# Third stage of a four-layer graph network: feed-forward and head scores in fp32r passes over parts, residual by transposes, end of the layer norm on VectorE, last attention first in the step

## The chip, the cores and the metric

One core of one Trainium2 chip. The metric is the time of one execution in device microseconds; the median of three runs is given beside the lowest and the highest. TensorE multiplies, VectorE, ScalarE and GpSimd work on SBUF (the first two on PSUM as well), SyncE issues the transfers.

## The reference

`x` is 64 graphs of 128 nodes with 256 features, `adj` one 128 x 128 matrix. Four residual blocks run one after the other, each on `h = relu(layernorm(x))`: an attention with 8 heads, a linear mixing with degrees, a graph attention with 4 heads and feed-forward (the third stage, which the change touches), and a graph attention with one head.

```python
def heads(x, adj, W, a):                       # W: [H, F, O], a: [H, 2O]
    Wh = einsum('bnf,hfo->bhno', x, W)
    f1 = einsum('bhno,ho->bhn', Wh, a[:, :O])
    f2 = einsum('bhno,ho->bhn', Wh, a[:, O:])
    e = f1[:, :, :, None] + f2[:, :, None, :]
    e = where(e > 0, e, 0.01 * e)
    e = where(adj > 0, e, -1e9)
    return einsum('bhnm,bhmo->bhno', softmax(e), Wh)

h = elu(heads(h, adj, W_heads, a_heads))       # 4 heads of 256
out = elu(heads(h.reshape(B, N, 1024), adj, W_out, a_out))
y = relu(out @ w1 + b1) @ w2 + b2 + out
x = x + layernorm(y) * ln_gamma + ln_beta
```

## The kernel before

All of `x` lies in SBUF (`x_all`). Every stage works through 32 groups of two graphs (G = 2) in a software pipeline: `run_steps` calls the stage's step function for t = -2 up to 35, and within a step each engine has a fixed, hand-written order of pieces that belong to different groups. In the third stage (`step2` of each engine) the pieces have a lag: `f` (group t) transposes h, forms the head features and scores of the four heads; `m` (group t-1) is the softmax's transposes and the four heads' attention; `o2` (t-2) is the product with W_out; `l` (t-3) is the last attention and the first feed-forward product; `e` (t-4) is the second feed-forward product, the residual and the layer norm. Only steps 4 to 31 hold all five. Engines meet by semaphores alone; there is no planner.

Large products run in fp32r over parts: an operand w is split into `w_hi` (a copy rounded to fp32r) and `w_lo` (the rest), and hi*hi + lo*hi + hi*lo are summed in PSUM, three passes in the place of one fp32 product (L1324 projections, L1350 W_out, L1311 features). In the trace an fp32 product shows as two matmul records. The feed-forward products (L1433, L1372) and the head scores (L1393) are plain fp32.

TensorE's order in a step before: transposes of h (L1141), transposes of probs (L1366), second feed-forward product with uT as the stationary operand (L1372) and the residual, outT times the identity (L1374), features, head(0) and head(1) (L1337), head scores with the mask (L1390, L1393), last scores (L1147, L1401), out_product(0) and (1) (L1350), project(0) (L1324), head(2), transposes of the last probabilities (L1412), out_product(2), head(3), last attention (L1422), project(1), out_product(3), first feed-forward product (L1433). PSUM bank 7 is used by the last scores, the last attention, both feed-forward products and y in turn, so each piece waits until the one before it was read.

VectorE's pieces: `hT2_lo` (L721), low_head (L697), y from bank 7 plus b2 (L729), `left`, `right_rows`, `right` for the head scores (L735, L736, L739), elu_head (L690, L692), bn_stats and bn_aggr (L746, L756; L248, L263 for the next h), soft (L702, L704), the last softmax (L760, L762, L769, L772), normalise (L708, L710), the ELU of the last attention `em3` and `outT` (L793, L797), the scaling of y (L784), `wh2` (L717). ScalarE's: `hT2_hi` (L997), probsT (L993), high_head (L973), exp_head (L966), scores_out (L979), exp_scores (L985), project_out (L960), h (L291), the last attention's copies and exponentials (L1017, L1026, L1042, L1058), uT (L1073). GpSimd does the square roots (L277, L489), adds beta to x (L304), multiplies y by gamma (L494) and adds it to x (L497).

Of the kernel before, what the change touches and what calls it, by code (L numbers as in the profile page):

```python
# [13 lines left out]
FP32 = mybir.dt.float32  # L14
# [55 lines left out]
def build_program(nc, x, adj, L0_gnn_Wq, L0_gnn_bq, L0_gnn_Wk, L0_gnn_bk, L0_gnn_Wv, L0_gnn_bv, L0_gnn_Wo,  # L70
# [10 lines left out]
    with ctx:  # L81
# [10 lines left out]
        ffn2 = sb("ffn2", [N, KC, D])  # L92
        w3 = sb("w3", [N, KC, F3 + 2])
        consts = sb("consts", [N, N + 4 + H2 * N])
# [3 lines left out]
        head_rows = consts[:, N + 4:].rearrange("p (h n) -> p h n", h=H2)  # L98
# [16 lines left out]
        bv_wide = sb("bv_wide", [N, KC, N])  # L115
# [17 lines left out]
        hT = sb("hT", [N, KC, G, N])  # L133
# [7 lines left out]
        rwide0 = sb("rwide0", [N, 4, 4 * DH])  # L141

        left = sb("left", [64, N])
        right_rows = sb("right_rows", [64, N])
        right = sb("right", [64, H2, N])
# [10 lines left out]
        em3 = sb("em3", [N, KC, G, N])  # L156
        outT = sb("outT", [N, KC, G, N])
        uT = sb("uT", [N, KC, G, N])
        y = sb("y", [N, G, D])
# [4 lines left out]
        h3 = sb("h3", [N, 4, G, F3 + 2])  # L164
# [6 lines left out]
        with ExitStack() as early:  # L171
# [6 lines left out]
            with ExitStack() as layer0:  # L178
# [10 lines left out]
                att0T = sb_0("att0T", [N, KC, G, N])  # L189
            with ExitStack() as layer1:  # L190
# [14 lines left out]
        wf_hi = sb("wf_hi", [N, KC, 3 * DH], F32R)  # L205
        wf_lo = sb("wf_lo", [N, KC, 3 * DH], F32R)
# [8 lines left out]
        a3_rows = h3[:, 0, :, 0:F3]  # L215
# [156 lines left out]
        u_full = sem("u_full")  # L372
        u_ready = sem("u_ready")
        y_full = sem("y_full")
# [3 lines left out]
        yg_ready = sem("yg_ready")  # L378
# [53 lines left out]
        LATE_DONE = 4 + 4 * H2 + 8 + 4  # L432
# [21 lines left out]
        def _(pool):  # L454
# [25 lines left out]
            if PHASES > 2:  # L480
                pool.wait_ge(pre[1].x, NG)

                def step2(at):
# [23 lines left out]
        def _(dve):  # L507
# [45 lines left out]
            def late_part(i):  # L553
# [8 lines left out]
                if i in (1, 2):  # L562
                    s = i - 1
                    for hh in range(H2):
                        late(nc.vector.tensor_tensor(prod4, wh[:, :, hh, :], av[:, hh, s:s + 1, :].broadcast_to([N, KC, D]), ALU.mult))
                        late(nc.vector.reduce_sum(wh_f[:, :, s * H2 + hh], prod4, AX.X))
                if i in (0, 3):
# [113 lines left out]
            def step2(at):  # L681
# [41 lines left out]
                if o2:  # L723
                    low_head(3, go)
                if e:
                    dve.wait_ge(y_full, ge + 1)
                    if positive(ge):
                        dve.wait_ge(pre[2].x, ge)
                    nc.vector.tensor_tensor(y[:, :], bank[7][:, :].rearrange("p (c d) -> p c d", c=G),  # L729
                                            b2_row[:, :, :].broadcast_to([N, G, D]), ALU.add).then_inc(y_step, 1)  # L730
                if f:
# [6 lines left out]
                    dve.wait_ge(lr_step, g * 2 + 1)  # L738
                    nc.vector.tensor_tensor(right[:, :, :], right_rows[:, :].unsqueeze(1).broadcast_to([64, H2, N]),  # L739
                                            head_rows[0:64], ALU.mult).then_inc(lr_step, 1)  # L740
                if m:
                    elu_head(0)
                if e:
# [3 lines left out]
                    last.then_inc(y_step, 1)  # L747
                if m:
# [9 lines left out]
                if l:  # L758
                    dve.wait_ge(scores3, gl + 1)
                    nc.vector.scalar_tensor_tensor(t3[:, 0], t3[:, 0], LEAK2, t3[:, 0], ALU.mult, ALU.max).then_inc(top3, 1)  # L760
                    dve.wait_ge(top3, gl * 2 + 1)
                    nc.vector.tensor_reduce(negtop[:, :], t3[:, 0], AX.X, ALU.max, negate=True).then_inc(top3, 1)  # L762
# [4 lines left out]
                if l:  # L767
                    dve.wait_ge(exp3, gl + 1)
                    nc.vector.reciprocal(rsum3[:, :], sum3[:, 0, :]).then_inc(rsum3_ready, 1)  # L769
                    dve.wait_ge(rsum3_ready, gl + 1)  # L770
                    for c in range(G):
                        last = nc.vector.tensor_scalar(t3[:, 0, c, :], t3[:, 0, c, :], rsum3[:, c:c + 1], None, ALU.mult)  # L772
                    last.then_inc(p3_ready, 1)
                if f:
                    normalise(0)
                moments_dve(2, at)
                if m:
                    low_head(0, gm)
                    low_head(1, gm)
                    elu_head(2)  # L780
                if e:
                    dve.wait_ge(y_norm, ge * 2 + 2)
                    for c in range(G):
# [3 lines left out]
                if f:  # L787
                    normalise(1)
                if m:
                    elu_head(3)  # L790
# [728 lines left out]
```

## Time and profile before

| | us |
|---|---|
| median of 3 runs | 1637.37 (1637.23 to 1638.43) |
| the profiled execution | 1637.47 |
| its span | 1635.7 |
| TensorE busy | 1449.0 (89%) |
| VectorE busy | 1202.6 (74%) |
| ScalarE busy | 1024.2 (63%) |
| GpSimd busy | 454.5 (28%) |

Busy time is the union of an engine's instructions, as a share of the span. Durations of matmuls are pipelined: two that follow one another overlap, so the time that one occupies is read from start to start. A row of a timeline merges a few like instructions (x8) and gives in brackets the idle time before it and what ended it.

### The profile page before, as it was taken

Reading aid. Unit: us, or ns where it says so; the run is one execution under the profiler, and the core shown is the slowest. Engines: PE = TensorE matmul, PEld = TensorE weight load, DVE = VectorE, ACT = ScalarE, POOL = GpSimd, SP = SyncE. Lnnn points to the kernel's source line nnn. Section 1 sums busy time; section 2 is a strip of 40 time slices with the busy share of each in tenths; the row PEclk is TensorE's granted clock in tenths of the full one; section 3 lists DMA queues with packets and bytes.
Section 4 is the critical chain, followed back from the end, with each engine's and each line's share of the span. In section 5 each row is a group of like instructions: output and inputs, shape, how many; then the busy total and the mean of one; then the engine's idle time right before and its main releaser. Section 6 shows DMA issues by size and latency. Waiting matters only on the chain.

```text
span 1635.7 us, 36230 instructions
## 1 busy us (share of the span) xinstructions
PE 1449.0 (89%) x11581; PEld 1276.4 (78%) x11645; DVE 1202.6 (74%) x2747; ACT 1024.2 (63%) x3241; POOL 454.5 (28%) x747
## 2 busy tenths in 40 slices
PE   5689999999879987999999999999999999965776
PEld 4578888888769985888888888888888888854554
DVE  4877777767657766777878787787878778743887
ACT  3568878878735546666656566665656666522776
POOL 1122222222036652122223132222313222122332
PEclk9889999999969997999999999999999999996999
DMA  7400000000000000000000000000000000000112
GB/s 238 136 2 0 0 0 0 0 0 0 1 1 0 0 0 1 1 1 1 1 0 0 0 0 0 0 0 0 0 0 0 0 0 1 1 1 7 65 64 71
DMA packets 23873, 24.23 MB, mean 15 GB/s; under 512 B 1936, under 2 KB 23184, under 8 KB 23696
## 3 DMA queue, kind: packets, MB, share of 16 engines
q1 hardware_dynamic: 23824, 23.60, 4.6%
q8 instruction: 27, 0.44, 0.1%
q14 instruction: 22, 0.18, 0.0%
HBM read 15.21 MB, written 8.39 MB: 14 GB/s over the span
## 4 chain that ended last, share of the span: by engine, by line
PE 43%; DVE 26%; ACT 17%; issue 12%; DVEq 1%; POOL 1%; DMA 0%; ACTq 0%; SPq 0%; POOLq 0%
ACT probs L877 9%; PE bank L1433 4%; DVE em L690 4%; PE bank L1337 4%; PE bank L1372 4%; PE bank L1141 3%; DVE probs L702 2%; PE bank L1234 2%; PE bank L1225 2%; DVE st L248 2%; PE bank L1393 2%; PE bank L1266 2%; PE bank L1279 2%; PE bank L1278 2%; PE bank L1280 2%
## 5 line engine op out<-in xcount | busy, mean ns | idle before, releaser
L877 ACT ACTIVATE probs<-bank,negtop 128x128 f32<-128x128 f32 x512 | 185.8, 415 | 48.0 <-DVE negtop L630 48.0
L275 POOL TENSOR_TENSOR var_eps<-mv,eps_tile 128x2 f32<-128x2 f32 x128 | 48.5, 379 | 590.7 <-DVE mv L263 590.7
L291 ACT ACTIVATE h<-x_all,shift,rstd 128x256 f32 (+1 forms) x256 | 140.0, 597 | 33.1 <-POOL shift L281 33.1
L1350 PE MATMUL bank<-wout_hi,headsT_hi 128*128 128x258 f32 x512 | 150.5, 294 | 0.0
L1350 PE MATMUL bank<-wout_lo,headsT_hi 128*128 128x258 f32 x512 | 144.4, 282 | 0.0
L1350 PE MATMUL bank<-wout_hi,headsT_lo 128*128 128x258 f32 x512 | 144.2, 282 | 0.0
L966 ACT ACTIVATE em<-bank 128x512 f32<-128x512 f32 x128 | 75.7, 591 | 98.9 <-PE bank L1337 98.5
L487 POOL TENSOR_TENSOR var_y<-mv_y,eps_tile 128x2 f32<-128x2 f32 x32 | 8.8, 276 | 463.1 <-DVE mv_y L756 463.1
L1337 PE MATMUL bank<-probsT,whs 128*128 128x128 f32 x1024 | 132.8, 278 | 0.0
L877 ACT ACTIVATION_READ_ACCUMULATOR probs<-bank,negtop 128x1 f32 x512 | 130.0, 254 | 0.0
L1337 PEld LDWEIGHTS bank<-probsT,whs 128*128 128x128 f32 x1024 | 125.9, 194 | 2.7
L985 ACT ACTIVATE probs<-probs,negtop 128x128 f32<-128x128 f32 x256 | 99.9, 394 | 27.8 <-DVE negtop L704 27.8
L690 DVE TENSOR_SCALAR em<-em 128x512 f32<-128x512 f32 x128 | 85.2, 666 | 33.4 <-ACT em L966 29.9
L277 POOL TENSOR_TENSOR rstd<-var_eps,pow_half 128x2 f32<-128x2 f32 x128 | 104.6, 818 | 10.0
L1324 PE MATMUL bank<-wh_hi,hT_hi 128*128 128x512 f32 x256 | 104.7, 409 | 1.4 <-ACT probs L979 1.4
L1183 PE MATMUL bank<-consts,probs 128*128 128x128 f32 x512 | 75.3, 280 | 31.6 <-DVE probsT L586 17.1
L1324 PE MATMUL bank<-wh_hi,hT_lo 128*128 128x512 f32 x256 | 101.8, 398 | 0.0
L1433 PE MATMUL bank<-outT,ffn 128*128 128x256 f32 x256 | 65.5, 400 | 40.8 <-DVE outT L797 40.8
L1324 PE MATMUL bank<-wh_lo,hT_hi 128*128 128x512 f32 x256 | 101.6, 397 | 0.0
L1350 PEld LDWEIGHTS bank<-wout_hi,headsT_hi 128*128 128x128 f32 x512 | 96.8, 189 | 2.4 <-issue 0.8
L1350 PEld LDWEIGHTS bank<-wout_lo,headsT_hi 128*128 128x128 f32 x512 | 97.2, 190 | 1.2
L627 DVE TENSOR_REDUCE negtop<-bank 128x4 f32<-128x512 f32 x128 | 88.4, 690 | 12.1 <-PE bank L1234 12.1
(215 smaller groups left out, 4638.3 us busy)
## 6 DMA issues: line engine op xcount, KB each, us to landing
x_all<-in_x SPq DMA_DIRECT2D x32, 256.0 KB, 2.8
out_x<-x_all SPq DMA_DIRECT2D x32, 256.0 KB, 2.1
wh<-in_L_gnn_W_heads SPq DMA_DIRECT2D x2, 512.0 KB, 7.9
a_heads<-in_L_gnn_a_heads SPq DMA_DIRECT2D x1, 1024.0 KB, 11.1
wout<-in_L_gnn_W_out SPq DMA_DIRECT2D x1, 1024.0 KB, 10.8
raw<-in_L_gnn_W SPq DMA_DIRECT2D x1, 512.0 KB, 5.3
ffn<-in_L_gnn_w SPq DMA_DIRECT2D x2, 256.0 KB, 7.2
consts<-in_shape_consts SPq DMA_DIRECT2D x1, 322.0 KB, 2.8
```

What stands on the lines that cost most here:

```text
L277: nc.gpsimd.tensor_tensor(rstd[:, p, :], var_eps[:, p, :], pow_half[:, :], ALU.pow).then_inc(s.norm, 1)
L291: last = nc.scalar.activation(h[:, p, c, :], x_all[:, bass.ds(g * G + c, 1), :].rearrange("p a d -> p (a d)"), ACT.Relu, bias=shift[:, p, ...
L627: nc.vector.tensor_reduce(negtop0[:, r, :], bank[4 + r][:, :].rearrange("p (k n) -> p k n", k=4), AX.X, ALU.max, negate=True).then_inc(top ...
L690: nc.vector.tensor_scalar(em[:, i % 2], em[:, i % 2], 1.0, -1.0, ALU.min, ALU.add).then_inc(hd2_elu, 1)
L877: last = nc.scalar.activation(probs[:, r, i, :], bank[4 + r][:, i * N:(i + 1) * N], ACT.Exp, bias=negtop0[:, r, i:i + 1], scale=float(DH) ...
L966: nc.scalar.activation(em[:, i % 2], bank[3 + i % 2][:, :].rearrange("p (k n) -> p k n", k=KC), ACT.Exp).then_inc(hd2_exp, 1)
L985: last = nc.scalar.activation(probs[:, c, hh, :], probs[:, c, hh, :], ACT.Exp, bias=negtop2[:, c, hh:hh + 1], accum_out=sum2[:, c, hh:hh + 1])
L1183: last = nc.tensor.transpose(bank[2 + r % 2][:, k * N:(k + 1) * N], probs[:, r, k, :], ident)
L1324: last = nc.tensor.matmul(bank[1 + half][:, :], src[:, k, c, :], w[:, k, 2 * half:2 * half + 2, :].rearrange("p h o -> p (h o)"), start=(k ...
L1337: last = nc.tensor.matmul(bank[3 + i % 2][:, (o * G + c) * N:(o * G + c + 1) * N], whs[:, pm, c, i * D + o * N:i * D + (o + 1) * N], probs ...
L1350: last = nc.tensor.matmul(bank[5 + c][:, 0:D + 2], src[:, i, o, c, :], w[:, k, :], start=(k == 0 and src is headsT_hi and w is wout_hi), s ...
L1433: last = nc.tensor.matmul(bank[7][:, o * G * N:(o + 1) * G * N], ffn1[:, k, o * N:(o + 1) * N], outT[:, k].rearrange("p c n -> p (c n)"), ...
```

## The change

Five things are done to the third stage.

1. ffn1 and ffn2 are split once into hi and lo (in steps 0 and 1, ScalarE the copy, VectorE the rest). `outT` and `uT` are split in every step by VectorE. Both feed-forward products become three fp32r passes each.
2. The residual is four fp32 transposes of outT into bank 7 ahead of the second product, which adds to it; it waits for `uT` alone, the product for its parts.
3. Head scores: the features' weight columns stand twice, so that the 16 rows hold f and f again; VectorE takes `f_high` (rounded), forms `f_part` (f_high in the first rows, f - f_high in the others), and from that `left`, `right_rows` and `right` in fp32r. The product with them is one fp32r pass per graph.
4. The end of the layer norm goes to VectorE: (y - mean) * gamma, then times rstd plus x, each a scalar_tensor_tensor per graph. GpSimd keeps the square roots and the beta add.
5. Order. TensorE: last scores between head(0) and head(1), last probabilities' transposes after out_product(1), last attention after project(0), first feed-forward product ahead of out_product(3). VectorE and ScalarE follow with the pieces of `l` earlier, and exp_scores(0) behind both high_heads, project_out(0) and (1) behind exp_scores(1). The loop's buffers `em3`, `uT`, `outT`, `y` now lie in unused quarters of probs and probsT, `h3` and `hT` in whs.

```diff
 # gpsimd, step2
-                    if there:
-                        pool.wait_ge(yn_ready, g + 1)
-                        nc.gpsimd.tensor_tensor(y[:, :], y[:, :], gamma_row[:, :, :].broadcast_to([N, G, D]),
-                                                ALU.mult).then_inc(yg_ready, 1)
-                        pool.wait_ge(yg_ready, g + 1)
-                        nc.gpsimd.tensor_tensor(x_group(g), x_group(g), y[:, :], ALU.add).then_inc(pre[2].x, 1)
 # vector, step2
-                    nc.vector.tensor_scalar(left[:, :], bank[0][0:64, 0:N], left_mul[0:64], left_add[0:64], ALU.mult, ALU.add)
-                    nc.vector.tensor_scalar(right_rows[:, :], bank[0][0:64, 0:N], right_mul[0:64], right_add[0:64],
+                    nc.vector.tensor_copy(f_high[:, :], bank[0][0:64, 0:N]).then_inc(lr_step, 1)
+                    dve.wait_ge(lr_step, g * 4 + 1)
+                    nc.vector.scalar_tensor_tensor(f_part[:, :], f_high[:, :].bitcast(FP32), low_rows[0:64], bank[0][0:64, 0:N],
+                                                   ALU.mult, ALU.add).then_inc(lr_step, 1)
+                    dve.wait_ge(lr_step, g * 4 + 2)
+                    nc.vector.tensor_scalar(left[:, :], f_part[:, :], left_mul[0:64], left_add[0:64], ALU.mult, ALU.add)
+                    nc.vector.tensor_scalar(right_rows[:, :], f_part[:, :], right_mul[0:64], right_add[0:64],
                                             ALU.mult, ALU.add).then_inc(lr_step, 1)
...
-                if e:
-                    dve.wait_ge(y_norm, ge * 2 + 2)
-                    for c in range(G):
-                        last = nc.vector.tensor_scalar(y[:, c, :], y[:, c, :], mv_y[:, c, 0:1], rstd_y[:, c:c + 1],
-                                                       ALU.subtract, ALU.mult)
-                    last.then_inc(yn_ready, 1)
...
+                    dve.wait_ge(at3_elu, gl * 2 + 2)
+                    nc.vector.tensor_copy(outT_hi[:, :, :, :], outT[:, :, :, :]).then_inc(outT_ready, 1)
+                    dve.wait_ge(outT_ready, gl * 2 + 1)
+                    nc.vector.tensor_tensor(outT_lo[:, :, :, :], outT[:, :, :, :], outT_hi[:, :, :, :].bitcast(FP32),
+                                            ALU.subtract).then_inc(outT_ready, 1)
+                if f:
+                    normalise(0)
+                if m:
+                    elu_head(2)
+                if f:
+                    normalise(1)
+                if m:
+                    elu_head(3)
                     low_head(2, gm)
+                if l:
+                    dve.wait_ge(u_relu, gl + 1)
+                    nc.vector.tensor_copy(uT_hi[:, :, :, :], uT[:, :, :, :]).then_inc(u_ready, 1)
+                    dve.wait_ge(u_ready, gl * 2 + 1)
+                    nc.vector.tensor_tensor(uT_lo[:, :, :, :], uT[:, :, :, :], uT_hi[:, :, :, :].bitcast(FP32),
+                                            ALU.subtract).then_inc(u_ready, 1)
+                if e:
+                    dve.wait_ge(y_step, ge * 3 + 3)
+                    for c in range(G):
+                        last = nc.vector.scalar_tensor_tensor(y[:, c, :], y[:, c, :], mv_y[:, c, 0:1], gamma_row[:, 0, :],
+                                                              ALU.subtract, ALU.mult)
+                    last.then_inc(yn_ready, 1)
+                    dve.wait_ge(yn_ready, ge + 1)
+                    dve.wait_ge(y_norm, ge * 2 + 2)
+                    dve.wait_ge(pre[2].bias, ge + 1)
+                    for c in range(G):
+                        xs = x_all[:, bass.ds(ge * G + c, 1), :].rearrange("p a d -> p (a d)")
+                        last = nc.vector.scalar_tensor_tensor(xs, y[:, c, :], rstd_y[:, c:c + 1], xs, ALU.mult, ALU.add)
+                    last.then_inc(pre[2].x, 1)
 # tensor, step2
+                def residual():
+                    pe.wait_ge(u_relu, ge + 1)
+                    for c in range(G):
+                        for k in range(KC):
+                            nc.tensor.matmul(bank[7][:, c * D + k * N:c * D + (k + 1) * N], outT[:, k, c, :], ident, is_transpose=True,
+                                             start=(c == 0 and k == 0), stop=False)
+
+                def second_ffn():
+                    pe.wait_ge(u_ready, ge * 2 + 2)
+                    for c in range(G):
+                        for k in range(KC):
+                            for src, w in ((uT_hi, ffn2_hi), (uT_hi, ffn2_lo), (uT_lo, ffn2_hi)):
+                                last = nc.tensor.matmul(bank[7][:, c * D:(c + 1) * D], src[:, k, c, :], w[:, k, :], start=False,
+                                                        stop=(c == G - 1 and k == KC - 1 and src is uT_lo))
+                    last.then_inc(y_full, 1)
...
+                def first_ffn():
+                    if not positive(gl):
+                        pe.wait_ge(w_lo, 5)
+                    pe.wait_ge(outT_ready, gl * 2 + 2)
+                    for o in range(KC):
+                        for k in range(KC):
+                            for w, src in ((ffn1_hi, outT_hi), (ffn1_lo, outT_hi), (ffn1_hi, outT_lo)):
...
```

## Rows read from the trace of the kernel before

**Rows 1.** Busy time by engine in one stretch of the third stage:
```profile
core 0: us, PE busy (x) PEld busy (x) DVE busy (x) ACT busy (x) POOL busy (x), PEclk, DMA share, GB/s
700.00:1300.00 600.00, 567.62 (x3928) 501.66 (x3950) 481.73 (x993) 376.93 (x1059) 167.13 (x207) 1.00 0.00 0
```

**Rows 2.** Timeline of GpSimd over one step, start us and length us first:
```profile
1000.66 1.29 POOL L494 TENSOR_TENSOR y<-y,gamma_row 128x512 f32<-128x512 f32 x1 [1.40 <-DVE y L784]
1002.14 1.50 POOL L497 TENSOR_TENSOR x_all<-x_all,y 128x512 f32 x1 [0.19 <-POOL y L494]
...
1019.55 1.42 POOL L304 TENSOR_TENSOR x_all<-x_all,beta_row 128x512 f32 x1
...
1026.68 1.29 POOL L494 TENSOR_TENSOR y<-y,gamma_row 128x512 f32<-128x512 f32 x1 [1.40 <-DVE y L784]
```

**Rows 3.** Two lines of the third stage: count, ns min/median/max, first and last start:
```profile
L721 DVE TENSOR_TENSOR hT_lo<-bank,hT_hi x32: 682/692/692, 617.5 to 1399.4; 128x512 fp32r<-128x512 f32 x32
...
L729 DVE TENSOR_TENSOR y<-bank,b_row x32: 690/692/693, 699.6 to 1481.7; 128x512 f32<-128x512 f32 x32
```

**Rows 4.** Waits between 700 and 1300 us: total, times, longest:
```profile
ACT uT L1073 <- PE bank L1433: 67.5, 23, 3.0
DVE hT_lo L721 <- ACT hT_hi L997: 57.5, 23, 2.5
...
PE bank L1433 <- DVE outT L797: 30.3, 23, 1.3
```

**Rows 5.** Timeline of TensorE over one step:
```profile
1005.77 1.99 PE L1433 MATMUL bank<-outT,ffn 128*128 128x256 f32 x8 [1.33 <-DVE outT L797]
1007.60 0.60 PE L1141 MATMUL bank<-consts,h 128*128 128x128 f32 x4
...
1008.91 1.03 PE L1372 MATMUL bank<-ffn,uT 128*128 128x256 f32 x4
...
1011.45 0.30 PE L1311 MATMUL bank<-hT_hi,wf_hi 128*64 128x128 f32 x1
...
1014.65 1.13 PE L1393 MATMUL bank<-right,left 32*128 32x512 f32 x4
1015.71 0.43 PE L1147 MATMUL bank<-consts,wh 128*128 128x128 f32 x2
...
1016.01 0.36 PE L1350 MATMUL bank<-wout_hi,headsT_hi 128*128 128x258 f32 x1
...
1018.96 0.39 PE L1324 MATMUL bank<-wh_hi,hT_hi 128*128 128x512 f32 x1
```

**Rows 6.** Timeline of VectorE over one step:
```profile
999.86 0.73 DVE L784 TENSOR_SCALAR y<-y,mv_y,rstd_y 128x256 f32<-128x256 f32 x2
...
1000.71 1.79 DVE L710 TENSOR_TENSOR probs<-probs,rsum 128x512 f32<-128x512 f32 x1
1002.42 1.51 DVE L690 TENSOR_SCALAR em<-em 128x512 f32<-128x512 f32 x1
...
1004.57 0.42 DVE L793 TENSOR_SCALAR em<-em 128x512 f32<-128x512 f32 x1
...
1012.55 0.40 DVE L735 TENSOR_SCALAR left<-bank,consts 64x128 f32<-64x128 f32 x1
...
1018.36 0.40 DVE L760 SCALAR_TENSOR_TENSOR t<-t 128x256 f32<-128x256 f32 x1
...
1021.42 0.48 DVE L772 TENSOR_SCALAR t<-t,rsum 128x128 f32<-128x128 f32 x2
...
1022.02 0.69 DVE L710 TENSOR_TENSOR probs<-probs,rsum 128x512 f32<-128x512 f32 x1
```

**Rows 7.** Group of a line in the set-up: count, busy us, mean ns, idle before:
```profile
L531 DVE CAST wkT_hi<-bank 128x512 fp32r<-128x512 f32 x1 | 0.7, 692 | 0.0
```

**Rows 8.** Chain that ended last, in the drain of the third stage:
```profile
1477.07 2.08 PE bank L1372 x4
...
1481.72 0.70 DVE y L729
...
1485.38 1.27 POOL y L494
```

More of the change, by code:

```diff
@@ L140, in build_program @@
         rsum0 = sb("rsum0", [N, 4, 4])
-        rwide0 = sb("rwide0", [N, 4, 4 * DH])
-        left = sb("left", [64, N])
+        left = sb("left", [64, N], F32R)
+        f_high = sb("f_high", [64, N], F32R)
+        f_part = sb("f_part", [64, N])
         right_rows = sb("right_rows", [64, N])
-        right = sb("right", [64, H2, N])
+        right = sb("right", [64, H2, N], F32R)
         negtop2 = sb("negtop2", [N, G, H2])
@@ L155, in build_program @@
         p3T = sb("p3T", [N, G, N])
[L156 to L159, printed above, removed]
+        outT_hi, outT_lo, uT_hi, uT_lo = [sb(name, [N, KC, G, N], F32R) for name in ("outT_hi", "outT_lo", "uT_hi", "uT_lo")]
         st_y = sb("st_y", [N, G, 6])
@@ L730, in step2 @@
                                             b2_row[:, :, :].broadcast_to([N, G, D]), ALU.add).then_inc(y_step, 1)
+                if o2:
+                    low_head(3, go)
                 if f:
@@ L810, in step2 @@
                     nc.vector.tensor_tensor(flat(wout_lo), flat(wout), flat(wout_hi).bitcast(FP32), ALU.subtract).then_inc(w_lo, 1)
+                if isinstance(at.t, int) and at.t == 1:
+                    for i, (w, hi, lo) in enumerate(((ffn1, ffn1_hi, ffn1_lo), (ffn2, ffn2_hi, ffn2_lo))):
+                        dve.wait_ge(w_hi, 4 + i)
+                        nc.vector.tensor_tensor(flat(lo), flat(w), flat(hi).bitcast(FP32), ALU.subtract).then_inc(w_lo, 1)
             if PHASES > 2:
@@ L1050, in step2 @@
                         nc.scalar.copy(hi, w).then_inc(w_hi, 1)
+                if n and isinstance(gn, int) and gn == 1:
+                    for hi, w in ((ffn1_hi, ffn1), (ffn2_hi, ffn2)):
+                        nc.scalar.copy(flat(hi), flat(w)).then_inc(w_hi, 1)
                 if m:
@@ new lines, in scores @@
+                def scores():
+                    pe.wait_ge(lr_step, g * 4 + 4)
+                    if positive(g):
+                        pe.wait_ge(whs_ready, g * 4)
+                    for c in range(G):
+                        nc.tensor.matmul(bank[1 + c][:, :], ident_bf[:, :], hide2[:, :, :], start=True, stop=False)
+                    for c in range(G):
+                        rows = slice(c * 32, (c + 1) * 32)
+                        nc.tensor.matmul(bank[1 + c][:, :], left[rows, :], right[rows].rearrange("p h n -> p (h n)"),
+                                         start=False, stop=True).then_inc(s2_full, 1)
@@ new lines, in scores_last, with probs_last @@
+                def scores_last():
+                    pe.wait_ge(wh2_act, gl + 1)
+                    pe.wait_ge(wh2_dve, gl + 1)
+                    if positive(gl):
+                        pe.wait_ge(y_step, gl * 3 - 2)
+                    neighbours(bank[7], wh2[:, pl, :, D + 1:D + 2], stop=False)
+                    nc.tensor.matmul(bank[7][:, 0:G * N], ident_bf[:, :], hide2[:, 0:G, :], start=False, stop=True).then_inc(s3_full, 1)
+                def probs_last():
+                    pe.wait_ge(p3_ready, gl + 1)
+                    for c in range(G):
+                        last = nc.tensor.transpose(bank[7][:, c * N:(c + 1) * N], t3[:, 0, c, :], ident)
+                    last.then_inc(pT3_full, 1)
@@ new lines, in attend_last @@
+                def attend_last():
+                    pe.wait_ge(pT3_ready, gl + 1)
+                    for o in range(KC):
+                        for c in range(G):
+                            last = nc.tensor.matmul(bank[7][:, (o * G + c) * N:(o * G + c + 1) * N], wh2[:, pl, c, o * N:(o + 1) * N],
+                                                    p3T[:, c, :], start=True, stop=True)
+                    last.then_inc(at3_full, 1)
+                def first_ffn():
+                    if not positive(gl):
+                        pe.wait_ge(w_lo, 5)
+                    pe.wait_ge(outT_ready, gl * 2 + 2)
+                    for o in range(KC):
+                        for k in range(KC):
+                            for w, src in ((ffn1_hi, outT_hi), (ffn1_lo, outT_hi), (ffn1_hi, outT_lo)):
+                                last = nc.tensor.matmul(bank[7][:, o * G * N:(o + 1) * G * N], w[:, k, o * N:(o + 1) * N],
+                                                        src[:, k].rearrange("p c n -> p (c n)"),
+                                                        start=(k == 0 and w is ffn1_hi and src is outT_hi), stop=(k == KC - 1 and src is outT_lo))
+                    last.then_inc(u_full, 1)
@@ L1368, in step2 @@
                 if e:
-                    pe.wait_ge(u_ready, ge + 1)
-                    for c in range(G):
-                        for k in range(KC):
-                            nc.tensor.matmul(bank[7][:, c * D:(c + 1) * D], uT[:, k, c, :], ffn2[:, k, :], start=(k == 0), stop=False)
-                        for k in range(KC):
-                            last = nc.tensor.matmul(bank[7][:, c * D + k * N:c * D + (k + 1) * N], outT[:, k, c, :], ident,
-                                                    start=False, stop=(k == KC - 1))
-                    last.then_inc(y_full, 1)
+                    residual()
+                    second_ffn()
                 if f:
```

182 lines of the change are left out of this document (82 added, 100 removed).

## The prediction

> **What bounds the kernel now.** I read the windows by stage first. The third stage runs from about 617 to 1488 us, and in its settled middle (700 to 1300 us) TensorE is busy 567.62 of 600 us, VectorE 481.73 and ScalarE 376.93 [rows 1]. Next the timeline of GpSimd, which gives the beat: the gamma product starts at 1000.66 and again at 1026.68 [rows 2], so a step takes 26.02 us, and the 600 us hold 23.06 steps. Per step that is TensorE 24.6 us, VectorE 20.9, ScalarE 16.3. The steps that do everything are steps 4 to 31, 28 of them: the last split of hT starts at 1399.4, in step 31, and 27 beats before it lie at 696.9, just ahead of the first y add at 699.6 [rows 3]. Next the waits [rows 4]: TensorE's one regular wait is for outT ahead of the first feed-forward product, 30.3 us in 23 steps, 1.3 us each. VectorE waits 2.5 us a step for ScalarE's hT_hi, which itself is queued behind uT, for which ScalarE waits 2.9 us on that same product. So the bound is TensorE's queue plus one hole per step, which the chain attention 3 -> outT -> first product -> uT makes at the end of the step. Last the timeline of TensorE, for what each piece occupies [rows 5], and that of VectorE [rows 6]. There two instructions stand out: the normalising product takes 1.79 us at 1000.71 but 0.69 at 1022.02, and the em clamp takes 1.51 at 1002.42 while the like clamp of em3 takes 0.42 at 1004.57 [rows 6]. Each long one ends 0.3 to 0.55 us after a GpSimd product of 512 columns that runs over it (ends at 1001.95 and 1003.64) [rows 2, 6]. VectorE thus loses 1.10 + 1.09 = 2.2 us a step to GpSimd.
>
> **The change part by part: TensorE.** I count from start to start, since the pipelined durations overlap. 24 passes in fp32r of 258 columns take 18.96 - 16.01 = 2.95 us, 0.123 each [rows 5].
> - First product: 7.60 - 5.77 = 1.83 us now; 12 passes of 256 columns give 1.47. Minus 0.36.
> - Second product with residual: 11.45 - 8.91 = 2.54 now. After: 12 passes, 1.47, and 4 transposes; the step's four transposes of h and eight of probs lie between 1007.60 and 1008.91, 0.11 each, so 0.44. Minus 0.63.
> - Head scores: 15.71 - 14.65 = 1.06 now. Two fp32r products of 512 columns on 32 rows aren't in the trace. From below: the two, which stand on different partitions, run wholly beside one another, 0.25; from above: no gain, 1.06. I take two passes behind one another at twice the price of a 256-column one, 0.49. Minus 0.57 (0 to 0.8).
> - The hole of 1.33: the last attention is now begun before the head sums, so outT has more than a step's half to be formed and split. It goes, if VectorE keeps up (below).
> TensorE's step: 26.02 - 1.33 - 0.36 - 0.63 - 0.57 = 23.1 us (22.9 to 23.7).
>
> **VectorE**, from 20.9:
> - Scores by parts: f_high and f_part read PSUM like `left` now (0.40) and each is waited for by the next, so 0.43 each; left and right_rows then read SBUF, where a 128-column scaling costs about 0.28 (the pair at 1021.42 takes 0.48) instead of 0.40 [rows 6]. Plus 0.6 (0.4 to 0.9).
> - Splitting outT and uT: per tile a cast of 512 columns from SBUF to fp32r and a subtraction. The subtraction is like the two-tensor product at 1022.02, 0.69. The cast isn't in the trace. From below: the clamp of 512 columns, SBUF to SBUF, 0.42; from above: a cast from PSUM to fp32r, 0.69 [rows 7]. I take 0.43, since it is the same movement as the clamp, SBUF to SBUF with one tensor read. Plus 1.1 for each tile (to 1.4), 2.2 together.
> - Layer norm end: two scalings go (0.73 the pair, 0.65 by starts); four scalar_tensor_tensor of 256 columns come, the nearest 0.40 for 256, 0.35 by starts. Plus 0.75 (0.6 to 1.1).
> - GpSimd's product with gamma and its add to x go: minus 2.2 of VectorE's stalls. The add of beta stays, 1.42 us. Now it runs over a reduction and bn_stats, which it doesn't stretch. After the change the batch statistics of y end later, and the add falls on low_head(0), a two-tensor subtraction in SBUF, which by my walk is reached 0.65 us before the add ends: plus 0.65 (0 to 1.1).
> Sum: 20.9 + 0.6 + 2.2 + 0.75 - 2.2 + 0.65 = 22.9 us (21.9 to 24.6).
> The Trainium skill (SBUF — State Buffer, on the shared port pair) calls this pair an exclusive lock: the second of a two-input or fast-mode VectorE instruction and a GpSimd one blocks until the first is done. The trace agrees, with 1.79 against 0.69 us, and the rule gives both the stalls that go and the one that comes; if the length had another cause that stays, the sum would be 24.4. The Trainium skill (VectorE: DVE Perf Modes, the perf-mode tier table) gives an fp32 copy in SBUF the double rate but names no fp32r output; by it the casts would be nearer 0.43.
>
> **ScalarE** keeps its instructions, 16.3 us: it is only reordered. GpSimd loses two of its longest.
>
> **The walk of one step.** I laid the new order out by hand with these prices, each engine in its own order, each instruction after what it waits for, from TensorE's transposes of h at 0. For TensorE and the chain: splits of hT done 3.0 (VectorE still ends the previous layer norm until 2.4), second product 1.75 to 3.2, y read 4.1, features to 3.9, last scores at 4.9, `right` done 6.7, just when head(1) ends (6.45: 0.25 us of waiting), p3 ready 9.8 for transposes at 10.3, attention 13.3 to 14.2, em3 at 14.9, outT split by 18 or 18.6 for a product that TensorE reaches at 20.2; uT 22.6, its split until 23.8, which is 0.7 into the next step for a product at 1.75. VectorE's ends, without the stall by the beta add: y 4.1, low_head(3) 4.7, `right` 6.7, maximum of the last scores 7.5, elu_head(0) 8.5, bn_stats of y 9.1, p3 9.8, elu_head(1) 10.9, soft(0) and soft(1) 13.7, bn_stats of x 14.3, low_head(0) and (1) 15.7, outT and its parts 18.0, normalise(0) 18.8, elu_head(2) 19.9, normalise(1) 20.7, elu_head(3) 21.8, low_head(2) 22.3, parts of uT 23.8, end of the layer norm 25.1, wh2 25.4, the last three in the next step's time. Nothing of the moved chain is late, but VectorE runs with no more than 0.4 us of rest. What is late next is therefore VectorE and TensorE in turn: `hT2_lo` ahead of the features, `right` ahead of the scores. 23.1 and 22.9 with 0.3 of such mutual waiting: **a step of 23.4 us**. Queued behind `right` are the hide matmuls, both out products and project(0), so each delay there goes into the beat.
>
> **Fill and drain.** The fill gains 0.6 us a step on the scores and pays 0.8 for the parts in steps 0 and 1, where they are on the path, and a little for splitting ffn1 and ffn2 once; its products and holes gain as above where they have begun: minus 2 in all, an estimate. In the drain I follow the chain [rows 8]. The last step: second product with residual from 1477.07 to 1481.72 at the lower of the two clocks (four products in 2.08 us against 1.03 at 1008.91), 4.65; after it 12 passes at twice the pitch, 2.9, behind a split of 1.1, with the residual beside it: minus 0.6. Behind the square root on GpSimd the scalings (0.8), the gamma product (1.3) and the add (1.3) become one pair of 0.8: minus 2.7. The steps 33 and 34: splits 1.1 each, the second product 0.3 less with its split counted, the first product 0.4 to 1 less, and in 33 the attention no longer behind an out product (1.47 less 0.4 for the copy of p3T it hid): minus 1 for both. Step 32 loses its hole and a stretched clamp: minus 1.5. Together minus 6.
>
> **Sum.** 28 x (26.02 - 23.4) = 73, fill 2, drain 6: minus 81. The profiled execution took 1637.47 us (span 1635.7, so 1.8 outside), the median of the runs is 1637.37; the two are the same to 0.1 us. 1637.5 - 81 = **1556 us**.
>
> **The rivals.**
> 1. VectorE becomes the bound alone: casts at 0.69, scaling with two pointers at 0.40, the full stall by the beta add; the sum 24.6, or about 24.5. For it: 20.9 is already high and this engine gets 10 instructions and loses 2; against: the 2.2 us of stalls are measured. Time: 1637.5 - 28 x 1.5 - 8 = 1587.
> 2. VectorE has room, the scores overlap: TensorE's 22.9 alone. 1637.5 - 28 x 3.1 - 9 = 1542. Against: it wants all of VectorE's prices at their lower end.
> 3. Slower. Bank 7 is one buffer for the whole chain scores 3, attention 3, first product, second product, y; it is passed once a step, and the splits put 2.3 us and four instructions of a full VectorE queue into it. uT's split is behind low_head(2), the second product in front of the features. If it comes late, TensorE stands and everything behind it. The point where it decides: 0.7 into the step by my walk, harmless to 1.75, no gain left if it ends 2.9 us later than that, at 4.6. At 5.6 the beat is 27.0 and the time 1637.5 + 28 x 1.0 - 8 = 1657. Against: in the walk the chain's links are met by their engines with 1 to 2.2 us to spare.
> 4. The parts don't pay: fp32r on 32 rows is no faster than fp32. TensorE 23.7, a step of 23.9: 1570, inside the forecast's range.
>
> **How the numbers follow.** Forecast with rival 4 (a step of 23.1 to 24.0): 0.61. Rival 1: 0.24. Rival 2: 0.08. Rival 3: 0.04. Between 25.5 and 26.1 us a step, no measurable change: 0.03. Range 1538 to 1592: the bounds 22.9 and 24.6 of the two sums, with 2 us beyond; it leaves out rival 3, the no-change case and the tails. About 0.2%, 3 us, is what a measurement can tell from no change. Faster 0.93, same 0.03, slower 0.04.
>
> **What would show it.** The beat of the y add near 23.4. TensorE without a wait at the first product, with short ones at features or scores. VectorE above 95% busy. The normalising product and the clamps at 0.69 and 0.42 without long ones, and low_head(0) stretched under the beta add. The casts at 0.43. A cast at 0.69 or a wait of TensorE for the split of uT would make the prediction wrong.

## The result and the profile after

| | us |
|---|---|
| before, median | 1637.49 (1637.23 to 1638.43, 4 runs) |
| after, median | 1557.26 (1556.89 to 1557.59, 4 runs) |
| ratio | 0.9509, 95% interval 0.9493 to 0.9525 |
| the profiled execution after | 1557.43, span 1555.4 (1637.47 and 1635.7 before) |

The forecast was 1556. First the busy time in the same stretch as [rows 1], and GpSimd's timeline, which answers to [rows 2] (start, length, engine, line):

```profile
core 0: us, PE busy (x) PEld busy (x) DVE busy (x) ACT busy (x) POOL busy (x), PEclk, DMA share, GB/s
700.00:1300.00 600.00, 590.33 (x4399) 535.68 (x4398) 571.08 (x1300) 414.06 (x1176) 112.17 (x182) 1.00 0.00 0
```

```profile
1007.77 0.55 POOL L493 TENSOR_TENSOR var_y<-mv_y,eps_tile 128x2 f32<-128x2 f32 x1 [18.23 <-DVE mv_y L775]
1008.40 0.69 POOL L495 TENSOR_TENSOR rstd_y<-var_y,pow_half 128x2 f32<-128x2 f32 x1
1009.05 1.27 POOL L309 TENSOR_TENSOR x_all<-x_all,beta_row 128x512 f32 x1
...
1031.23 0.55 POOL L493 TENSOR_TENSOR var_y<-mv_y,eps_tile 128x2 f32<-128x2 f32 x1 [18.05 <-DVE mv_y L775]
...
1054.87 0.55 POOL L493 TENSOR_TENSOR var_y<-mv_y,eps_tile 128x2 f32<-128x2 f32 x1 [18.23 <-DVE mv_y L775]
```

The beat alternates between 23.46 and 23.64 us, 23.56 in the mean over eight steps, where it was 26.02. The 600 us hold 25.5 steps, so VectorE is busy 22.4 us of each and TensorE 23.2. The waits between 700 and 1300 us (total, times, longest) answer to [rows 4]:

```profile
ACT probs L1101 <- PE bank L1447: 31.0, 25, 1.3
...
PEld bank L1347 <- DVE hT_lo L723: 13.9, 25, 0.7
...
PE bank L1347 <- DVE hT_lo L723: 8.8, 25, 0.5
...
PEld bank L1412 <- DVE right L746: 5.6, 25, 0.3
```

TensorE no longer waits for outT. What is left in each step is 0.35 to 0.56 us for hT_lo ahead of the features (L1347; the first figure is that of the matmuls, the second that of the weight load) and 0.2 for `right` ahead of the scores (L1412). The timeline of TensorE answers to [rows 5]:

```profile
1002.66 0.50 PE L1415 MATMUL bank<-right,left 32*128 32x512 f32 x2
1003.09 0.39 PE L1386 MATMUL bank<-wout_hi,headsT_hi 128*128 128x258 f32 x1
...
1015.98 0.28 PE L1447 MATMUL bank<-outT_hi,ffn_hi 128*128 128x256 f32 x1
...
1017.41 0.28 PE L1386 MATMUL bank<-wout_hi,headsT_hi 128*128 128x258 f32 x1
...
1018.85 0.60 PE L1177 MATMUL bank<-consts,h 128*128 128x128 f32 x4
...
1020.16 0.60 PE L1395 MATMUL bank<-consts,probsT 128*128 128x128 f32 x4
...
1022.45 0.27 PE L1347 MATMUL bank<-hT_hi,wf_hi 128*64 128x128 f32 x1 [0.27 <-DVE hT_lo L723]
```

The scores take 0.43 us from start to start (1.06 before), the first product 1.43 (1.83 before). VectorE's timeline answers to [rows 6]:

```profile
1000.06 0.28 DVE L737 CAST f_high<-bank 64x128 fp32r<-64x128 f32 x1
1000.38 0.34 DVE L739 SCALAR_TENSOR_TENSOR f_part<-f_high,consts,bank 64x128 f32<-64x128 f32 x1
...
1009.68 1.19 DVE L699 TENSOR_TENSOR headsT_lo<-em,headsT_hi 128x512 fp32r<-128x512 f32 x1
...
1012.70 0.43 DVE L795 CAST outT_hi<-probsT 128x512 fp32r<-128x512 f32 x1
...
1015.85 0.69 DVE L712 TENSOR_TENSOR probs<-probs,rsum 128x512 f32<-128x512 f32 x1
1016.46 0.42 DVE L692 TENSOR_SCALAR em<-em 128x512 f32<-128x512 f32 x1
...
1018.49 0.43 DVE L810 CAST uT_hi<-probs 128x512 fp32r<-128x512 f32 x1 [0.28 <-ACT probs L1101]
1018.95 0.69 DVE L812 TENSOR_TENSOR uT_lo<-probs,uT_hi 128x512 fp32r<-128x512 f32 x1
1019.56 0.88 DVE L817 SCALAR_TENSOR_TENSOR probsT<-probsT,mv_y,gamma_row 128x256 f32<-128x256 f32 x2
1020.58 0.88 DVE L825 SCALAR_TENSOR_TENSOR x_all<-probsT,rstd_y,x_all 128x256 f32 x2
1021.38 0.42 DVE L719 COPY wh<-bank 128x258 f32<-128x258 f32 x1
1021.72 0.68 DVE L723 TENSOR_TENSOR hT_lo<-bank,hT_hi 128x512 fp32r<-128x512 f32 x1
```

The normalising product and the clamp that took 1.79 and 1.51 us take 0.69 and 0.42. low_head(0) takes 1.19 under the beta add, which ends at 1010.32. The last six rows are the piece that the experiments below turn on: VectorE waits for uT, splits it, ends the layer norm, copies wh2 and only then splits hT, at 1022.40; TensorE's features start 0.05 later.

### The profile page after: what moved, and what is told of

Same layout as the page of the kernel before. It is cut to its first block, busy times and chain, and to the rows that moved or that the text cites. A ratio compares the mean times of both kernels' runs of the same rounds, so it can differ in the third digit from the quotient of the medians.

```text
span 1555.4 us, 36699 instructions
## 1 busy us (share of the span) xinstructions
PE 1402.9 (90%) x11709; PEld 1253.6 (81%) x11709; DVE 1260.4 (81%) x3006; ACT 1021.1 (66%) x3243; POOL 364.0 (23%) x683
## 4 chain that ended last, share of the span: by engine, by line
PE 60%; DVE 16%; ACT 15%; issue 7%; DVEq 1%; POOL 1%; ACTq 0%; DMA 0%; SPq 0%; POOLq 0%
PE bank L1360 11%; ACT probs L907 9%; PE bank L1386 9%; PE bank L1373 7%; PE bank L1177 3%; PE bank L1447 3%; PE bank L1270 2%; PE bank L1261 2%; PE bank L1248 2%; PE bank L1436 2%; PE bank L1302 2%; PE bank L1314 2%; PE bank L1316 2%; PE bank L1315 2%; DVE negtop L629 2%
## 5 line engine op out<-in xcount | busy, mean ns | idle before, releaser
L493 POOL TENSOR_TENSOR var_y<-mv_y,eps_tile 128x2 f32<-128x2 f32 x32 | 16.6, 518 | 570.9 <-DVE mv_y L775 570.9
L1373 PE MATMUL bank<-probsT,whs 128*128 128x128 f32 x1024 | 136.2, 276 | 0.0
L699 DVE TENSOR_TENSOR headsT_lo<-em,headsT_hi 128x512 fp32r<-128x512 f32 x128 | 101.6, 795 | 1.3 <-ACT headsT_hi L1003 0.3
L282 POOL TENSOR_TENSOR rstd<-var_eps,pow_half 128x2 f32<-128x2 f32 x128 | 98.2, 768 | 10.0
L1386 PEld LDWEIGHTS bank<-wout_hi,headsT_lo 128*128 128x128 f32 x512 | 96.6, 189 | 0.0
L253 DVE BATCH_NORM_STATS2 st<-x_all 128x6 f32 (+1 forms) x256 | 95.0, 413 | 0.1
```

The costliest lines, as they stand in the source:

```text
L253: last = nc.vector.bn_stats(st[:, p, c, :], x_all[:, bass.ds(g * G + c, 1), :].rearrange("p a d -> p (a d)"))
L282: nc.gpsimd.tensor_tensor(rstd[:, p, :], var_eps[:, p, :], pow_half[:, :], ALU.pow).then_inc(s.norm, 1)
L699: nc.vector.tensor_tensor(headsT_lo[:, i].rearrange("p k c n -> p k (c n)"), em[:, i % 2], headsT_hi[:, i].rearrange("p k c n -> p k (c n) ...
L1373: last = nc.tensor.matmul(bank[3 + i % 2][:, (o * G + c) * N:(o * G + c + 1) * N], whs[:, pm, c, i * D + o * N:i * D + (o + 1) * N], probs ...
L1386: last = nc.tensor.matmul(bank[5 + c][:, 0:D + 2], src[:, i, o, c, :], w[:, k, :], start=(k == 0 and src is headsT_hi and w is wout_hi), s ...
```

## The experiments

Times are medians beside runs of the kernel before on the same chip, whose own median moved between 1636.6 and 1639.4, so the ratios compare. The beat is the mean distance of GpSimd's first operation on the statistics of y over six to eight steps of the profiled execution.

| kernel | us | ratio (95%) | beat |
|---|---|---|---|
| before | 1637.5 | 1 | 26.02 |
| after | 1557.3 | 0.9509 (0.9493 to 0.9525) | 23.56 |
| e1 layer norm end on GpSimd | 1603.0 | 0.9805 (0.9788 to 0.9823) | 25.10 |
| e2 feed-forward in fp32 | 1568.7 | 0.9585 (0.9567 to 0.9603) | 24.02 |
| e3 head scores in fp32 | 1567.2 | 0.9585 (0.9569 to 0.9601) | 23.99 |
| e4 the order alone | 1589.9 | 0.9722 (0.9706 to 0.9738) | 24.60 |
| e8 all but the order | 1642.2 | 1.0033 (1.0020 to 1.0045) | 26.21 |
| e5 beta add first | 1557.0 | 0.9512 (0.9493 to 0.9531) | 23.57 |
| e7 e5, uT_hi on ScalarE | 1566.3 | 0.9566 (0.9545 to 0.9586) | 23.92 |
| e6 both products two passes | 1541.1 | 0.9419 (0.9399 to 0.9440) | 23.18 |
| e9 second product two passes | 1555.6 | 0.9498 (0.9483 to 0.9513) | 23.57 |
| e10 first product two passes | 1545.2 | 0.9430 (0.9417 to 0.9444) | 23.18 |
| e11 e5, layer norm end halved | 1556.0 | 0.9494 (0.9480 to 0.9507) | 23.42 |
| e12 e5, layer norm end early | 1563.3 | 0.9545 (0.9530 to 0.9559) | 23.66 |

### One part undone at a time

**e1.** The lines of GpSimd and the scaling of y are those of the kernel before, the four scalar_tensor_tensor go.

```diff
+                        nc.gpsimd.tensor_tensor(y[:, :], y[:, :], gamma_row[:, :, :].broadcast_to([N, G, D]),
+                                                ALU.mult).then_inc(yg_ready, 1)
...
+                        nc.gpsimd.tensor_tensor(x_group(g), x_group(g), y[:, :], ALU.add).then_inc(pre[2].x, 1)
...
-                        last = nc.vector.scalar_tensor_tensor(y[:, c, :], y[:, c, :], mv_y[:, c, 0:1], gamma_row[:, 0, :],
-                                                              ALU.subtract, ALU.mult)
...
```

> Part 4 alone undone: GpSimd multiplies by gamma and adds to x again, VectorE scales y ahead of normalise(1) as before. Theory (VectorE is full in the changed kernel, 22.4 us busy of a beat of 23.5, so each us it gets lengthens the step): it loses four scalar_tensor_tensor (about 1.9 us from start to start), gains two scalings (0.65) and the two stalls by GpSimd (2.2): plus 0.95 us in 28 steps, 27 us, plus 2.7 at the end of the stage: about 1587 us, beat 24.5, a normalising product or clamp of 1.5 to 1.8 us in the timeline. Rival (TensorE alone sets the beat, VectorE's load is covered): only the end of the stage, 1560 us.

Measured 1603.0, more than either theory gave. VectorE's timeline of e1, then its wait for y and TensorE's waits:

```profile
1008.82 1.80 DVE L719 TENSOR_TENSOR probs<-probs,rsum 128x512 f32<-128x512 f32 x1
1010.54 1.51 DVE L699 TENSOR_SCALAR em<-em 128x512 f32<-128x512 f32 x1
```

```profile
DVE probsT L736 <- PE bank L1403: 21.2, 24, 0.9
...
PE bank L1463 <- DVE em L701: 17.0, 24, 0.7
...
PE bank L1403 <- DVE uT_lo L825: 12.2, 24, 0.5
PE bank L1412 <- DVE right L753: 11.0, 24, 0.5
```

The stalls are back to within 0.01 us (1.80 and 1.51; 1.79 and 1.51 in the kernel before). The beat is 1.54 longer where VectorE's balance said 0.95. The two stalls and the scaling of y (2.2 and 0.65 us) stand right ahead of elu_head(3), whose end frees the bank for the next step's transposes of probs (L1463), and TensorE waits there, at the second product and at the scores in turn. VectorE pays for that once more: it stands 0.9 us a step for y, which comes out of the delayed second product (L1403), and this wait was not in the balance. Of the gain this part is worth 46 us, 43 of them in the beat. That the stalls make the difference, and not the place of the scaling, is the likely reading, since they are the larger part; no run separates the two.

**e2 and e3.** In e2 both products read outT and uT in fp32, and the casts and subtractions of these on VectorE go; in e3 `left` and `right_rows` come from PSUM as before.

```diff
-                            for w, src in ((ffn1_hi, outT_hi), (ffn1_lo, outT_hi), (ffn1_hi, outT_lo)):
+                            last = nc.tensor.matmul(bank[7][:, o * G * N:(o + 1) * G * N], ffn1[:, k, o * N:(o + 1) * N],
+                                                    outT[:, k].rearrange("p c n -> p (c n)"), start=(k == 0), stop=(k == KC - 1))
```

> The fp32r feed-forward alone undone: both products are fp32 on outT and uT, no splits of these on VectorE; the residual stays by transposes. TensorE gets 0.36 + 0.27 = 0.63 us a step, VectorE loses about 2.2. Theory (both engines are within 0.5 us of the beat, TensorE's work being 22.95 of 23.55): the beat becomes TensorE's 23.6 with little waiting, so the time is the changed kernel's within -4 and +11 us, 1553 to 1568: the splitting buys nearly nothing by itself. Rival A (TensorE alone sets the beat): plus 0.63 x 28 = 18, 1575 us. Rival B (VectorE alone sets it): faster, down to 22.5 a step, 1530 us.

> The head scores by parts alone undone: left and right in fp32 straight from PSUM, product in fp32. TensorE plus 0.6 us a step, VectorE minus 0.6. Theory (both full): the beat moves by 0 to 0.4 us, 1557 to 1569 us. Rival A (TensorE alone): plus 17, 1574. Rival B (VectorE alone): minus 17, 1540.

Measured plus 11 and plus 10 us (1568.7, 1567.2), beats 24.02 and 23.99. Each fp32r part is worth about 0.45 us a step, less than the 0.6 us of TensorE that it saves. e3 is inside what the theory gave, e2 just beyond its edge.

**e4 and e8.** e4 has the new order and nothing else; e8 everything but the new order.

> Only the order of the pieces is the changed kernel's; feed-forward, head scores, residual and the end of the layer norm are as before. Theory (the hole of 1.33 us ahead of the first product is closed by the order, nothing else is late): beat 24.7 to 24.9, that is 28 x 1.2 = 34 us below the kernel before, and 1 in the drain: about 1602 us; VectorE then has 20.9 us of 24.7 and shows waits. Rival (the order gives nothing as long as the engines carry their old work, since the hole only moves): 1637 us.

> All parts of the change but the order: the three engines take their pieces in the order of the kernel before, the splits follow outT and uT, the new layer norm end stands where the scaling of y stood. Theory (the order closes the hole ahead of the first product, and the parts would make it longer by a split of 1.1 us in it): TensorE's work of 22.95 plus a hole of about 2 us and 0.3 at the second product, beat 25.3, time about 1612 us, with a wait of TensorE for outT of about 2 us each step. Rival (the gain is in the cheaper work, the order is worth little): about 1560 us.

e4 is 47 us faster than the kernel before, 12 more than expected: the order alone is 58% of the gain. 28 beats of 1.42 are 40 of the 47 us; the rest lies in the fill and the drain, for which the expectation had 1. Its beat of 24.60 is TensorE's own work, busy 599.81 of 600 us. e8 is 5 us *slower* than the kernel before, 30 more than the theory gave. Its waits:

```profile
DVE uT_hi L824 <- ACT probs L1105: 39.7, 23, 1.7
...
PE bank L1443 <- DVE outT_lo L816: 35.9, 23, 1.7
...
PE bank L1408 <- DVE right L746: 12.8, 22, 0.6
...
PE bank L1399 <- DVE uT_lo L826: 8.6, 23, 0.4
```

In the old order the hole ahead of the first product is 1.6 us instead of 1.3 (the split stands in it), VectorE stands 1.7 us for the relu at the step's end, and TensorE then waits at the second product (0.4) and for `right` (0.6) as well. So the parts, with 1.6 us less of TensorE's work, gain nothing there, and 33 us behind the order (e4 to after).

e1 and e4 show the same kind of tie between the parts. Both have the new order and the old end of the layer norm; e1 has the cheaper products besides, and is 13 us slower (1603.0 against 1589.9). With the stalls in place VectorE is busy 23.6 us a step in e1, against 21.2 in e4, and what the splits cost there is more than what TensorE saves.

### What sets the new beat

The prediction's reading was that both engines are full. e5 takes a little from VectorE, e6 from TensorE (e6, e9 and e10 leave out low-part passes of the products, so they compute less than the others).

```diff
 # e5, GpSimd
                         pool.wait_ge(y_step, g * 3 + 3)
+                    bias_pool(pool, 2, at, beta_row)
+                    if there:
                         nc.gpsimd.tensor_tensor(var_y[:, :], mv_y[:, :, 1], eps_tile[:, :], ALU.add).then_inc(y_norm, 1)
...
-                    bias_pool(pool, 2, at, beta_row)
 # e6, TensorE
-                            for src, w in ((uT_hi, ffn2_hi), (uT_hi, ffn2_lo), (uT_lo, ffn2_hi)):
+                            for src, w in ((uT_hi, ffn2_hi), (uT_hi, ffn2_lo)):
...
-                            for w, src in ((ffn1_hi, outT_hi), (ffn1_lo, outT_hi), (ffn1_hi, outT_lo)):
+                            for w, src in ((ffn1_hi, outT_hi), (ffn1_lo, outT_hi)):
```

> The changed kernel with GpSimd's beta add ahead of the two operations of the square root (behind the same wait for the statistics of y), so that it runs over the reduction and bn_stats and not over low_head(0), which it stretches from 0.68 to 1.19 us now. Theory (VectorE is full and feeds TensorE just late): low_head(0) takes 0.68 again, VectorE loses 0.5 us a step, the beat falls by 0.3 to 0.5, time 1543 to 1549 us. Rival (TensorE sets the beat of 23.54 and VectorE's load is covered): no change, 1557.

> Leaves out the third pass of both feed-forward products (the one with the low part of outT and of uT), 8 of 24 passes; VectorE still forms the low parts, so only TensorE's work falls, by 0.96 us a step. Theory (both engines within 0.6 us of the beat, VectorE at 22.4 busy with no idle time but short waits): the beat falls by no more than 0.3 us, 1548 to 1557 us, and TensorE's waits for hT_lo and right grow. Rival (TensorE sets the beat): minus 0.96 x 28 = 27, 1530 us.

e5 changed nothing. VectorE's timeline of e5:

```profile
1010.31 0.70 DVE L700 TENSOR_TENSOR headsT_lo<-em,headsT_hi 128x512 fp32r<-128x512 f32 x1
...
1017.66 0.68 DVE L700 TENSOR_TENSOR headsT_lo<-em,headsT_hi 128x512 fp32r<-128x512 f32 x1
1019.11 0.43 DVE L811 CAST uT_hi<-probs 128x512 fp32r<-128x512 f32 x1 [0.77 <-ACT probs L1102]
```

The stretched subtraction is 0.70 again, and the 0.5 us saved is idle time in front of uT's split, 0.77 where it was 0.28. VectorE was not the bound. e6 was faster by 16 us, more than its theory allowed and little more than half of what TensorE's saving would give, so TensorE's work alone is not the bound either. A loop fits: first product, relu on ScalarE, uT's split, layer norm end, wh2 and hT_lo on VectorE, features, and TensorE's whole order up to the first product again. The second product lies beside VectorE's part of it. e7 to e12 test that.

> e5 and, besides, uT_hi written by ScalarE from PSUM by a second relu instead of by a cast on VectorE: VectorE another 0.46 us a step less, ScalarE 0.73 more (17.5 of 23), the residual waits for both. Theory: VectorE leaves the bound (21.4), the beat is TensorE's work of 22.95 plus 0.1: 23.05, time 1543 us, at most 3 us below e5. Rival (VectorE alone sets the beat): another 13 us below e5.

e7 came out at 1566, 9 us slower than e5, where its theory said 1543, though VectorE had less to do: the second relu of 0.73 us stands in the loop in the place of a cast of 0.46, and the beat grew by 0.35.

> Leaves out the third pass (low part of uT) of the second feed-forward product alone, 4 passes, 0.48 us of TensorE's work a step; VectorE forms the low part all the same. New theory (a loop sets the beat: first product, relu on ScalarE, split of uT, end of the layer norm, wh2 and hT2_lo in VectorE's queue, features and all of TensorE's order up to the first product; the second product lies beside VectorE's part of it, not in it): the 0.48 turns into a longer wait for hT_lo ahead of the features, 0.36 to 0.84 us, and the time stays at 1555 to 1558. Rival (TensorE's work sets the beat): minus 0.48 x 28 = 13, 1544 us.

> Leaves out the third pass (low part of outT) of the first feed-forward product alone, the same 0.48 us of TensorE's work, but inside the loop. New theory: minus 0.48 x 28 = 13, 1544 us, the wait for hT_lo unchanged near 0.36. Rival (VectorE is full and sets the beat): 1555 to 1558. TensorE alone as the bound would give 1544 here and in e9 too.

The same four passes, 0.48 us of TensorE's work, left out of one product or of the other. In e9 the beat is 23.57, unchanged, in e10 it is 23.18, and e6, without both, has 23.18 as well. The waits of e9 and of e10 for hT_lo:

```profile
PE bank L1347 <- DVE hT_lo L723: 20.7, 25, 0.9
```

```profile
PE bank L1347 <- DVE hT_lo L723: 11.6, 26, 0.6
```

In e9 the 0.48 has become waiting (0.83 us a step against 0.35). That settles, for the changed kernel, the loop against "TensorE's work" and against "VectorE is full". The beat of e10 fell by 0.38 and not by 0.48, though, and e6 with four passes fewer fell no further. VectorE's timeline of e10 says why:

```profile
1009.67 0.68 DVE L699 TENSOR_TENSOR headsT_lo<-em,headsT_hi 128x512 fp32r<-128x512 f32 x1
1010.27 0.42 DVE L810 CAST uT_hi<-probs 128x512 fp32r<-128x512 f32 x1
```

From the last low_head to the split of uT it takes 0.60 us, where the changed kernel takes 0.97: the relu is early now, the wait for it is gone, and no wait of VectorE for another engine is left in the step. So its queue, run through without a rest, takes 23.18 us and is the next bound, 0.38 below the loop. e6 ends at the same bound, and its second saving too becomes waiting for hT_lo (0.92 us a step, 0.45 in e10). Beside their own runs of the kernel before, e6 and e10 don't differ beyond their intervals; of e10 the profiled execution, from which its beat is read, took 1540.3 us and the four others 1545.2 to 1545.8.

**e11 and e12** try to shorten VectorE's part of the loop, the first by moving the pair (y - mean) * gamma ahead of uT's split, the second by moving both pairs.

> e5 (beta add first) with the first pair of the layer norm's end, (y - mean) * gamma, moved ahead of the split of uT, into the 0.77 us that VectorE waits there for the relu in e5; the second pair stays behind it. New theory: VectorE's part of the loop gets 0.8 us shorter, the wait for hT_lo (0.35 to 0.55) goes, the second product's end takes over as what the features wait for: beat down by 0.3 to 0.45, time 1544 to 1549 us. Rival (TensorE's work of 22.95 and its short waits have another cause than the loop): 1557.

> e5 with both pairs of the layer norm's end ahead of the split of uT. New theory: the split starts 1.0 us later than in e5 and the second product waits for it, some 0.2 us; its end, 0.3 us before where the features start in e5, sets the features: time 1547 to 1553 us, between e5 and e11. Rival (VectorE's total is what counts, not the place): as e11.

In e11 the wait for hT_lo is gone, as expected, but the beat fell by 0.15 only (0.3 to 0.45 expected) and the time by 1 us, inside the intervals. The waits of e11:

```profile
DVE probsT L730 <- PE bank L1405: 22.1, 25, 0.9
...
PE bank L1414 <- DVE right L747: 17.6, 26, 0.7
```

A second path, almost as long, took over: the second product's end, VectorE's add of y, low_head(3), the five instructions up to `right`, the scores. VectorE stands 0.9 us for y, and TensorE waits 0.7 for `right` where it was 0.2. e12 was expected between e11 and e5 and is 6 us slower than after, with a beat of 23.66: so the expectation was wrong, and no run shows which link failed. Its profiled execution took 1557.0 and the five others 1562.2 to 1565.1. Part of such differences lies ahead of the third stage, in work that no version changes: in the fourteen profiled executions its first split of hT starts anywhere from 612.9 (e12) to 618.9 us (e11), after at 615.5. From that split to the start of the last add to x it is 789.7 us in after, 786.6 in e11, 793.2 in e12 and 776.6 in e10, in step with the beats. Why the five other executions of e12 took longer stays open. None of the versions with the full computation beats the changed kernel beyond its interval.

## Why the prediction was right, point by point

- **The beat and the sum.** Forecast were 23.4 us and 73 us for 28 steps; measured 23.56, 28 x 2.46 = 69. The fill was forecast at 2 and gave 3.1 (from the first split of hT to the full steps), the drain at 6 and gave 8.2 (from the last split of hT to the last add to x: 88.6 us before, 77.9 after, less one beat's 2.46). The span is 80.3 shorter, the forecast said 81; part of that closeness is that two small errors of opposite sign met. Besides, the third stage began 2.0 us earlier (already so in the first stage, which the change leaves alone) and the fourth was 2.0 longer, its first 32 us at a mean granted clock of 0.61 of full speed against 0.74 before.
- **TensorE's terms.** First product 1.43 (forecast 1.47), residual and second product 1.86 (1.91), scores 0.43 (0.49, bounds 0.25 and 1.06). Work without waits 23.0 (23.1). Rival 4 is out. The scores' figure was near, but its picture was not: the two products do start together and lie beside one another in the records, and still cost about as much as two in a row (last section).
- **VectorE's terms.** Casts to fp32r from SBUF at 0.43, the value taken between 0.42 and 0.69. f_high cheaper than the forecast 0.43 (0.32 from start to start), the layer norm's instructions dearer: 0.48 each instead of 0.40. The stall that comes was 0.51 (0.65), the two that go went. Sum 22.4 (22.9).
- **The order closes the hole.** Right, and more than 1.33 us: e4 gives 1.42. But the prediction priced it as one term among five; e8 shows that it is a condition for the others, and e1 beside e4 that the end of the stalls is another.
- **What is late next.** The walk named hT2_lo ahead of the features and `right` ahead of the scores, and both are what the trace shows. The step that was wrong is the reason given. "VectorE runs with no more than 0.4 us of rest" is true as a size (0.38, by e10), but the total of its work does not set the beat: e5 took 0.5 us of its work away for nothing, e7 0.46 more for a loss. What counts is the stretch of its queue between uT and hT_lo, within the loop. That the number came out all the same is partly luck: the loop is only 0.38 us longer than VectorE's queue and 0.6 longer than TensorE's work, so a sum of either with a little waiting lands near it.
- **The stalls by GpSimd.** The Trainium skill (SBUF — State Buffer, on the shared port pair) has the second of the two blocked until the first is done. The trace agrees: in the changed kernel low_head(0) ends at 1010.87, 0.55 behind the beta add, and in e5, where the add runs over other instructions, it takes 0.70. e1 brings both old stalls back.

## What to carry to other kernels

Where the two busiest engines, each with a fixed order, are both above 90% busy, look for the loop that passes through several engines once a step, and ask of each saving whether it lies in it: the same four matmul passes were worth 0.38 us a step in one place and nothing in the other. Ask too how far below the next bound lies: here VectorE's queue cut the 0.48 us saved to 0.38, and in e11 a second path cut the gain to 0.15. In this kernel cheaper work behind a hole only made the hole longer (e8); closing it by order came first. Work moved to a less busy engine can still cost if it lands in the loop (e7), and work moved to a nearly full one can pay if it ends a contention (e1).

## What the runs showed of the hardware

- An fp32 to fp32r cast of 512 columns in SBUF takes 0.43 us on VectorE, one from PSUM 0.69 [rows 7].
- A scalar_tensor_tensor of 256 columns with a scalar per partition and two tensors in SBUF takes 0.48 us; with a constant and one tensor read twice it took 0.40 [rows 6].
- Two fp32r products of 32 rows and 512 columns on different partitions start together in the records and run beside one another: the 25 pairs of the window take 12.5 us, 0.50 a pair, and each of the two is 0.495 long, where a pass of 128 rows and 512 columns is 0.395. There is next to no gain in it: the next product starts 0.43 us after the pair, and two passes of 128 rows in a row take 0.47. The two groups of TensorE in the changed kernel, 700 to 1300 us (count, busy us, mean ns):

```profile
L1360 PE MATMUL bank<-wh_lo,hT_hi 128*128 128x512 f32 x208 | 82.1, 395 | 0.0
...
L1415 PE MATMUL bank<-right,left 32*128 32x512 f32 x50 | 12.5, 495 | 0.0
```

- The beta add on GpSimd takes 1.27 us in the changed kernel and 1.42 before; in e5 it takes 1.52, begun 0.37 us before the end of a scalar_tensor_tensor of VectorE. That fits GpSimd waiting for VectorE too.
